# Value product of a head pair in six matmuls with high and low parts side by side, its sums on VectorE, and a new order of the projections inside a batch

## The reference

```python
# block 0: 16 heads of 64; this is the part that the change touches
q = (layernorm(x) @ w_q).reshape(B, 112, 16, 64)
k, v = split(context @ w_kv)                      # both (B, 375, 16, 64)
attn = softmax(einsum('bqhd,bkhd->bhqk', q * SCALE, k))
out = einsum('bhqk,bkhd->bqhd', attn, v).reshape(B, 112, 1024) @ w_out + b_out
x = x + gates * out                               # then the spectral layer (x @ one folded matrix)
# block 1: one-head attention over the same context, then a mixture of 16 experts, 4 a token:
gate = softmax(top4(n @ gate_w)); x = x + sum(gate_e * expert_e(n))
```

## Time and profile before

| | us |
|---|---|
| median of 3 runs (lowest, highest) | 1104.79 (1103.99, 1105.89) |
| the profiled execution | 1109.83 |
| its span (first to last instruction) | 1108.1 |
| TensorE busy in the span | 1039.2 |
| VectorE busy | 803.5 |
| ScalarE busy | 714.7 |
| GpSimd busy | 516.6 |

### The profile page before, as it was taken

One profiled execution on the slowest core, in us unless ns is written; L12 is line 12 of the kernel. 1 busy time (PEld: TensorE's weight loads), 2 busy tenths in 40 slices (PEclk: granted clock), 3 DMA queues, 4 the chain that ended last, 5 costly groups with the idle time before them and its releaser, 6 DMA issues. The chain is left out here.

```text
span 1108.1 us, 22305 instructions
## 1 busy us (share of the span) xinstructions
PE 1039.2 (94%) x7055; PEld 961.0 (87%) x7055; DVE 803.5 (73%) x2017; ACT 714.7 (65%) x1853; POOL 516.6 (47%) x628
## 2 busy tenths in 40 slices
...
DMA packets 79840, 98.46 MB, mean 89 GB/s; under 512 B 14939, under 2 KB 71901, under 8 KB 79728
## 3 DMA queue, kind: packets, MB, share of 16 engines
...
...
## 5 line engine op out<-in xcount | busy, mean ns | idle before, releaser
L942 POOL TENSOR_TENSOR prob<-prob,rinv 112x750 f32<-112x750 f32 x128 | 184.1, 1438 | 251.1 <-DVE rinv L1614 250.7
L1032 ACT ACTIVATE prob<-ps_s,negmax 112x375 f32<-112x375 f32 x256 | 144.0, 570 | 59.7 <-DVE negmax L1608 56.9
L1621 DVE TENSOR_TENSOR pT_lo<-ps_pt,pT_hi 125x672 fp32r<-125x672 f32 x128 | 108.6, 848 | 64.1 <-ACT pT_hi L1169 64.1
L1712 PE MATMUL ps_kv<-ctxT_hi,wkv 128*128 128x376 f32 x512 | 138.4, 351 | 2.4 <-DVE v_lo L1281 1.2
L1608 DVE TENSOR_REDUCE negmax<-ps_s 112x2 f32<-112x750 f32 x128 | 119.0, 930 | 4.4 <-PE ps_s L1960 4.3
L1712 PE MATMUL ps_kv<-wkv,ctxT_hi 128*125 128x512 f32 x384 | 111.5, 413 | 1.1 <-DVE k_low L1277 0.2
L1022 ACT ACTIVATE v_hi<-ps_kv 125x512 fp32r<-125x512 f32 x96 | 57.3, 597 | 82.9 <-PE ps_kv L1712 82.9
L1970 PE MATMUL ps_pt<-ident,prob 112*125 112x112 f32 x768 | 104.4, 273 | 2.3 <-POOL prob L942 2.3
L901 POOL DMA_INDIRECT places<-ysb,place_i x72 | 71.6, 994 | 71.7 <-ACT ysb L1105 59.7
L1169 ACT ACTIVATE pT_hi<-ps_pt 125x672 fp32r<-125x672 f32 x128 | 93.6, 731 | 7.0 <-PE ps_pt L1970 1.1
L1960 PE MATMUL ps_s<-kx,qx_hi 128*112 128x376 f32 x256 | 94.1, 367 | 3.5 <-DMA kx<-k_low 2.6
...
## 6 DMA issues: line engine op xcount, KB each, us to landing
kx<-k_low SPq DMA_DIRECT2D x256, 94.0 KB, 2.2
...
```

What stands on the lines that cost most here:

```text
L942: e_prob.done(eng.tensor_tensor(prob[0:TQ, p % 2, :, :], prob[0:TQ, p % 2, :, :], rinv[:, 2 * p:2 * p + 2].unsqueeze(2).broadcast_to([TQ, ...
L1032: e_exp.done(eng.activation(prob[0:TQ, p % 2, half, :], S[0:TQ, half, 0:SK], ACT.Exp, bias=negmax[:, h:h + 1], accum_out=rowsum[:, h:h + 1]))
L1621: e_pt_lo.done(eng.tensor_tensor(pT_lo[:, :, :, :].rearrange("p h k t -> p h (k t)"), PT[0:KEYT, :, 0:NKEY * TQ], pT_hi[:, :, :, :].bitcas ...
L1712: last = eng.matmul(out_, lhs(i, k), rhs(j, k), start=(n == 1), stop=(n == KT * len(PASSES)))
```

## The change

Four things change.

1. **Layout.** `v_hi` and `v_lo` become one tensor `vx` in which each head has its 64 high and 64 low columns side by side; `pT_hi` and `pT_lo` become two halves of `pTx`.
2. **Value product.** Per pair six matmuls in place of nine, three for each head: stationary side 128 columns (high and low of one head), moving side 224 columns (high and low probabilities of that head). The result has four blocks; low by low is not used, the other three are to be added. ScalarE copies one block row (64 by 224) to `o_sum`; VectorE adds high-by-high to it (64 by 224), then adds the third block, once for each head (64 by 112 each), into `oT`. TensorE waits for that (`e_oT`) before the next pair's O. On VectorE the three additions stand in each odd slot ahead of `pT_lo`.
3. **Order.** `KV_AT` is new. By slot (of 16), before: 0 v1; 1 k2; 2 v2; 3 q1, k3; 4 r; 5 k4; 6 v3; 7 k5, e; 9 v4, k6; 10 k7, v5; 11 x, c0; 12 c1; 13 q0, k0; 15 k1, v0. Now: 0 q1; 1 v1, k2; 2 v2; 3 k3; 4 r; 5 k4, v3; 7 k5, e; 8 v4; 9 k6; 10 x, v5; 11 k7, c0; 12 c1, q0; 13 k0; 15 k1, v0. (Within a slot in the order of the list: slot 9 before is v4 and then k6.) On VectorE the comparison of the gate's logits moves from the start of slot 3 to the end of slot 2, the ranking from the start to the end of slot 3, `normed` 0 from the end of slot 20 to the end of slot 21, `normed` 1 from slot 22 to 23, and the next input's normed row from slot 8 to 9.
4. **Buffers and loads.** `base_row` shares the buffer of `xm`, so GpSimd waits for the store of the row before (`f_base`). Two of the four first weight loads are issued by ScalarE in slot -4 instead of SyncE at the start.

```diff
-        v_hi = t("v_hi", [128, NKEY, INNER], F32R)
-        v_lo = t("v_lo", [128, NKEY, INNER], F32R)
+        vx = t("vx", [128, NKEY, NH, 2, DH], F32R)
-        pT_hi = t("pT_hi", [KEYT, 2, NKEY, TQ], F32R)
-        pT_lo = t("pT_lo", [KEYT, 2, NKEY, TQ], F32R)
+        pTx = t("pTx", [KEYT, 2, 2, NKEY, TQ], F32R)
+        pT_hi, pT_lo = (pTx[:, n, :, :, :] for n in range(2))
-        base_row = t("base_row", [TQ, D])
-        xm = t("xm", [TQ, D])
+        base_row = xm = t("xm", [TQ, D])
+        o_sum = t("o_sum", [64, 2, TQ])
...
-        KV_AT = (("v", 1, 0), ("x", 0, -5), ("k", 2, 1), ("q", 0, -3), ("r", 0, 36), ("k", 7, 10),
+        KV_AT = (("q", 1, 0), ("v", 1, 1), ("k", 2, 1), ("v", 2, 2), ("k", 3, 3), ("r", 0, 36), ("k", 4, 5),
...
-        AT_LN, AT_XN, AT_XB0 = -10, -8, 3
+        AT_LN, AT_XN, AT_XB0 = -10, -7, 3
...
@@ ScalarE, odd slots @@
                             e_o.wait_ge(eng, st, p + 1)
-                            for half in range(2):
-                                rows_ = slice(64 * half, 64 * half + 64)
-                                last = eng.activation(oT[rows_, p, :], OT[rows_, half * TQ:(half + 1) * TQ],
-                                                      ACT.Copy)
-                            e_oT.done(last)
+                            e_oT.wait_ge(eng, st, p)
+                            e_o_low.done(eng.activation(o_sum[:, :, :], O_ALL[64:128, :, 0, :], ACT.Copy))
...
@@ VectorE, tail_end @@
-                tb = due(g, 20)
+                tb = also(g, 21, 20)
                 if tb:
                     e_rs_t.wait_ge(eng, tb, 1)
                     normed(tb, 0)
...
@@ VectorE, after tail(g) and ahead of pT_lo @@
+                    st = due(g, AT_O[p] + 1)
+                    if st:
+                        e_o_low.wait_ge(eng, st, p + 1)
+                        ct(eng.tensor_tensor(o_sum[:, :, :], O_ALL[0:64, :, 0, :], o_sum[:, :, :], ALU.add))
+                        ct.wait_ge()
+                        for half in range(2):
+                            last = eng.tensor_tensor(oT[64 * half:64 * half + 64, p, :], O_ALL[0:64, half, 1, :],
+                                                     o_sum[:, half, :], ALU.add)
+                        e_oT.done(last)
...
@@ TensorE @@
-                        for i, j in PASSES:
+                        for half in range(2):
                             for k in range(NKEY):
-                                last = eng.matmul(OT[:, 0:2 * TQ].rearrange("p (h t) -> p h t", t=TQ),
-                                                  vv[i][0:KEYT, k, p * 128:(p + 1) * 128],
-                                                  pT[j][:, :, k, :], start=(n == 1),
-                                                  stop=(n == NKEY * len(PASSES)))
+                                last = eng.matmul(O_ALL[:, half, :, :],
+                                                  vx[0:KEYT, k, 2 * p + half, :, :].rearrange("p j d -> p (j d)"),
+                                                  pTx[:, :, half, k, :], start=(k == 0), stop=(k == NKEY - 1))
```

102 lines of the change are left out of this document (53 added, 49 removed), and 3 rows, old and new, of the table KV_AT.

## The result

The changed kernel takes 1258.8 us (median of 4 runs, 1256.2 to 1262.1) where the kernel before takes 1105.3 beside it (1104.0 to 1107.7): 1.139 times as long, with a 95% interval of 1.135 to 1.142. That is 153 us more; I had forecast 55. A second set of runs gave 1259.7 against 1102.9, 1.143 [1.138, 1.148]. The profiled execution took 1259.7 us.

What follows compares the result with a forecast made beforehand. VectorE's occupied time (49.6 us a lap) passes TensorE's 48.9, and its remaining waits set the lap at 55.8. 14 laps x 4.2 less 3 gave +56 on 1104.8: 1161, predicted as 1160 us, range 1105 to 1182.

Steps and rivals of the forecast that it cites:

- the hops: VectorE's low part to the low part two jobs on, through TensorE and ScalarE: 2.5 us for v, 3.3 for q.
- both sides agree; I take 55.8 a lap: Lap counted twice, 56.1 us from VectorE and 56.2 from TensorE; 55.8 taken, +4.2 a lap.
- TensorE's side: Lap by TensorE: own need 48.9 us plus stalls of 8.3, less about 1 already standing: 56.2.
- VectorE's side: Lap by VectorE: occupied time 49.6 us plus waits that stay, 6.5: 56.1.
- q1's hop: Slots 15 to 0, k1's low part then q1: 3.3 us less v0's low part and negmax, a VectorE wait of 1.7.
- The balance has tipped: VectorE's occupied time, 41.6 + 8.0 = 49.6 us a lap, passes TensorE's 48.9, so its remaining waits count.
- A: Rival: TensorE stays the bound and gains 2.67 us a lap, 1062 us in all; chance 0.03.
- B: Rival: VectorE's occupied time is the bound, its waits vanish; lap 49.6 to 50.8, 1077 to 1094 us; chance 0.09.
- C: Rival: a wash, half the stalls real, +2.7 a lap against -2.67; 1103 to 1107 us; chance 0.04.
- D: Rival: slower by less, additions 0.75 us, VectorE not late everywhere; lap 52.3 to 54.6, 1112 to 1144 us; chance 0.24.
- F: Rival: worse, additions of 1.15 us and lag spilling between slots; lap 57 to 58.5, up to 1200 us; chance 0.07.
- Other edits: Outside the full laps: start -1 us, first batch element -2, stretch behind the last 0 (+1 and -1); f_base wait free.

Runs made afterwards that it cites:

- no_block: Changed kernel with two short VectorE pieces (layer norm's first refinement, reciprocal and product of sm1) moved ahead of rinv in their odd slots: 1242.2 us, ratio 1.097 to before.
- value_again: Kernel before, old order, with six value matmuls and no additions (three of four parts of O left out): 1089.0 us, ratio 0.988 to before.
- value_alone: Kernel before, old order, with the new value product, its copy and its three additions: 1185.2 us against 1135.3, ratio 1.042.
- order_alone: Kernel before with the new order only, old value product of nine matmuls and no additions: 1239.6 us against 1135.3, ratio 1.094.
- normed_old: Changed kernel with normed 0 and 1 moved back to slots 4 and 6: 1302.5 us, ratio 1.181 to before.
- v3_slot6: Changed kernel with v3 moved back from slot 5 to slot 6, between T1 and T2: 1301.7 us against 1129.1 before, ratio 1.153.
- fill_q1: Changed kernel plus 24 unread 128x64 matmuls on TensorE ahead of q1 in slot 0: 1276.1 us against 1135.3 before.
- fill_three: Changed kernel plus unread 128x64 matmuls in three TensorE stalls (17 before q1, 13 before T1, 15 before v5): 1268.5 us against 1128.5 before, ratio 1.123.

## Why the prediction was wrong

Direction and places were right. So were the value product (0.66 us), its additions (0.97), and the waits at the hops 1.2 for v2 (forecast 1.1), 1.1 for v5 (1.0), 2.1 for q0 (1.9), 0.8 for GpSimd (0.8).

*The step that failed* is "both sides agree; I take 55.8 a lap": the lap is 61.5 on the mean. By TensorE's side, which I put at 48.9 + 8.3 less 1:

- Its stalls are 10.8, not 8.3, counted as the prediction counted them, from start to start. The waits view shows 9.2: busy time runs until a matmul's result is out, and that hides about 0.16 us of each wait. The last matmul of S ahead of v4, and v4:

```profile
549.50 0.33 PE L1971 MATMUL ps_s<-kx,qx_lo 128*112 128x376 f32 x1
550.83 1.17 PE L1723 MATMUL ps_kv<-wkv,ctxT_hi 128*125 128x512 f32 x4 [1.00 <-DVE k_low L1268]
```

1.33 between the starts where 0.17 is usual: 1.16 lost for a wait of 1.00. So v5 lost 2.0 for 1.0 (behind the held instruction of slot 9; in no_block it waits 0.4), q1 with the S ahead of it 2.3 for 1.3, the others together 0.5 more than forecast: +2.5.
- What is left of the lap at the full clock is 48.6 (61.14 - 10.8 - 1.7), where 48.9 less 1 leaves 47.9: +0.7. The same count gives 50.7 before and 48.4 in value_again and in value_alone. So the product gave 2.3 of its 2.67, and 0.2 came with the order. (The lap of value_again gained only 1.3, since its own stalls grew from 1.0 to 1.9.)
- The slow clock, counted at nothing: +2.1. No rival had it either.

56.2 + 5.3 = 61.5. By VectorE's side, 49.6 + 6.5: q1's hop 3.5 for 1.7 (1.5 of it the clock: q1 held TensorE 3.24 us for 1.72), the other three hops +0.4, four small waits that I had not listed +1.5, the held instructions +2.5, the rest of its occupied time -1.2; together 61.1. That the two sides agreed at 56 was therefore no proof of either: both left out the clock, and each left out something of its own.

*The reason behind it was wrong as well.* "The balance has tipped, and what counts now is which of VectorE's waits stay" made VectorE's 8 us the condition and the order a detail. The runs show the reverse: the order costs 114 us without any addition, the additions 59 on the new order and about 66 on the old (1185.2 - 1135.3 + 16). Most of the stalls that I had found from TensorE's side (2.6 in slot 6, v4 1.1, c1 0.9, T7 0.6, and about half of v5's) were chains of their own: late low part, product, copy, low part. They don't need a full VectorE. q1's and the other half of v5's do: without additions they are 0.4 and 0.9, with them 2.2 and 1.9.

*Rivals.* A, B and C fell. Of A it is true that six matmuls gain, but 1.3 a lap, and only with the old order and without additions. D's reason, that VectorE is not late everywhere at once, is answered by order_alone: the stalls stand with a VectorE that is 70% busy. F came nearest, but its cause (additions of 1.15 us) was not the one.

*Other edits.* The start was not 3 us shorter: the first route transpose stands 14.1 later, of which 1.25 laps of +9.9 are 12. The last two stretches between writes of `route`, which reach past the last batch element, grew by 4.3 and 3.8 us (61.6 to 65.8, 67.4 to 71.1), and what follows the last route transpose by -1.2; for all of this I had 0.

Open: why in the changed kernel the clock fell at q1 or in slot 6 and not behind v5's stall of 1.9 (in normed_old and v3_slot6 it fell there too), and why fillers held it at q1 in fill_q1 and not in fill_three; and ScalarE's late start on one chip.
